# One shared PSUM bank in an attention kernel: its uses moved from the even step to the odd step behind the products with v, and a prologue over four banks

## The reference, cut to what matters

```python
x_proj = x @ Wqkv + bqkv                       # x is the normalised input, 512 tokens at a time
q = x_proj[:, :, :C].reshape(B, n_head, T, hd)          # n_head 16, hd 16: a reshape, not a transpose
k = x_proj[:, :, C:2 * C].reshape(B, n_head, T, hd)
v = x_proj[:, :, 2 * C:].reshape(B, n_head, T, hd)
att = jnp.einsum('bhtd,bhsd->bhts', q, k) * (1.0 / jnp.sqrt(jnp.float32(hd)))
att = jnp.where(causal, att, -jnp.inf)
att = jax.nn.softmax(att, axis=-1)
y = jnp.transpose(att @ v, (0, 2, 1, 3)).reshape(B, T, C)
out = y @ Wproj + bproj
```

## Time and profile before

| | us |
|---|---|
| median of 3 runs | 4216.47 |
| lowest and highest | 4213.61 to 4221.39 |
| the profiled execution, its own time | 4223.2 |
| its span, first to last instruction | 4221.3 |
| PE busy | 3870.2 |
| DVE busy | 2988.6 |
| ACT busy | 2260.9 |
| POOL busy | 1381.5 |

### The profile page before, as it was taken

One profiled execution on the slowest core, in us unless ns is written; L12 is line 12 of the kernel. 1 busy time (PEld: TensorE's weight loads), 2 busy tenths in 40 slices (PEclk: granted clock), 3 DMA queues, 4 the chain that ended last, 5 costly groups with the idle time before them and its releaser, 6 DMA issues. The chain is left out here.

```text
span 4221.3 us, 81220 instructions
## 1 busy us (share of the span) xinstructions
PE 3870.2 (92%) x28814; PEld 2530.1 (60%) x28814; DVE 2988.6 (71%) x7504; ACT 2260.9 (54%) x4454; POOL 1381.5 (33%) x1724
## 2 busy tenths in 40 slices
PE   4997899997499999999999999999999996899997
PEld 4886666674255555555555555555555553667664
DVE  6997467575287777777777777777778773457575
ACT  0110465664156666666666666566656664466664
POOL 2332142333524243243433324333343320133332
PEclk8999899998789999999999999999999998899999
DMA  1332111111677676866767766676666741112111
GB/s 56 99 99 95 40 61 60 51 51 53 115 96 121 101 102 104 114 104 100 116 100 115 107 105 109 94 116 100 103 108 102 101 73 47 41 51 64 47 56 45
DMA packets 701475, 361.54 MB, mean 86 GB/s; under 512 B 305072, under 2 KB 668080, under 8 KB 701104
## 3 DMA queue, kind: packets, MB, share of 16 engines
q1 hardware_dynamic: 701104, 356.65, 47.0%
HBM read 204.49 MB, written 150.99 MB: 84 GB/s over the span
## 5 line engine op out<-in xcount | busy, mean ns | idle before, releaser
L1583 DVE TENSOR_REDUCE att_maxima<-att_s 128x1 f32<-128x512 f32 (+3 forms) x3072 | 1523.1, 550 | 418.8 <-PE att_s L1759 222.7
L1681 ACT ACTIVATE att_probs<-att_s 128x512 f32<-128x512 f32 (+1 forms) x2560 | 1330.9, 556 | 892.4 <-PE att_s L1759 526.7
L1813 PE MATMUL att_s<-att_qs,att_ks 49*128 49x512 f32 (+3 forms) x3072 | 1005.3, 403 | 70.3 <-DVE att_maxima L1583 42.3
L1789 PE MATMUL att_s<-att_ks,att_qs 48*128 48x512 f32 (+3 forms) x3072 | 1003.2, 411 | 3.0 <-DVE att_maxima L1583 1.6
L1813 PEld LDWEIGHTS att_s<-att_qs,att_ks 49*128 49x128 f32 x3072 | 477.4, 187 | 631.2 <-ACT att_probs L1681 404.3
L1841 PE MATMUL att_o_ps<-att_probs,att_vs 128*32 128x512 f32 (+3 forms) x6144 | 638.3, 501 | 2.5 <-issue 2.0
L1759 PE MATMUL att_s<-att_mask,att_places 64*128 64x64 bf16 (+1 forms) x5632 | 595.3, 210 | 0.0
L1789 PEld LDWEIGHTS att_s<-att_ks,att_qs 48*128 48x128 f32 x3072 | 508.4, 189 | 16.8 <-DVE att_maxima L1583 8.6
L1057 PE MATMUL ffn_h2p<-ffn_h,ffn_w 128*128 128x512 f32 x768 | 365.5, 598 | 3.0 <-ACT ffn_h L938 0.9
L1759 PEld LDWEIGHTS att_s<-att_mask,att_places 64*128 64x128 bf16 x5632 | 285.9, 97 | 113.0 <-issue 42.8
L1500 POOL TENSOR_TENSOR att_x_res<-att_x_res,att_bp_row 128x512 f32<-128x512 f32 x64 | 81.3, 1280 | 756.8 <-DMA att_x_res<-x 755.4
(11 more groups left out here) (227 smaller groups left out, 5794.0 us busy)
## 6 DMA issues: line engine op xcount, KB each, us to landing
att_staged<-qk_scratch SPq DMA_DIRECT2D x768, 128.0 KB, 7.1
qk_scratch<-att_parts SPq DMA_DIRECT2D x128, 512.0 KB, 2.9
ffn_x<-x SPq DMA_DIRECT2D x64, 512.0 KB, 5.2
ssm_x<-in_L_attn_a_x_dram SPq DMA_DIRECT2D x32, 512.0 KB, 3.9
x<-ssm_y SPq DMA_DIRECT2D x32, 512.0 KB, 2.9
x<-ffn_y SPq DMA_DIRECT2D x32, 512.0 KB, 3.0
att_x<-x SPq DMA_DIRECT2D x32, 512.0 KB, 12.7
v_scratch<-att_v_tok SPq DMA_DIRECT2D x32, 512.0 KB, 3.5
```

The lines of the kernel that those rows point to most:

```text
L1583: last = v.tensor_reduce(maxima_of[p][:, g, blk, 1 if t0 else 0:2 if t0 else 1], s1_ps[(2 * unit + 1 - g) % 3][:, col:col + w], AX.X, ALU.max)
L1681: a(probs[u % 2][2 * g + p][:, 0:n], bank[:, 0:n], ACT.Exp).then_inc(exp_done, 1)
L1789: last = mm(bank[:, col:col + w], rows_of(qs[buf], g, KROWS, p, BT * blk, BT * (blk + 1)), rows_of(ks[buf], g, KROWS, p, t0, t1), start=k ...
L1813: last = mm(bank[:, col:col + w], rows_of(ks[buf], g, SHIFT + 1, p, BT * j, BT * (j + 1)), rows_of(qs[buf], g, SHIFT + 1, p, t0, t1), star ...
```

## The change

On PE, `slot` now makes the products with v first, and then, in the same place of the same odd step, the use of the x bank whose number is `at`. A use is therefore made between the halves g = 0 and g = 1 of step `at`, where it was between those of step at + 1. The task numbers of ACT, DVE, POOL and SP are not changed.

In the prologue the 22 uses rotate over four banks, `x_ps` and the three `s2_ps`, with counters of their own (`low_free`, `v_free`). The statistics and the normalising of the first two x pieces stand ahead of the weights (DVE, first piece only) and of the masks (POOL). The uses of hb 2 are put between the units of the first pass of quad 0, on PE and DVE. On SP the two `move_max` of quad 0 move behind the first and the last `store_part` of hb 2. On POOL `normalise(2, 0)` moves ahead of the second pair of `lay_out`.

```diff
+        prologue_ps = [x_ps, *s2_ps]
...
+        def x_bank(index):
+
+            return prologue_ps[index % len(prologue_ps)] if index < X_PROLOGUE else x_ps
+
...
-                sp.wait_ge(const_ready, 4)
                 for hb in range(3):
                     for j in range(4):
                         store_part(hb, hb % 2, j)
@@
                             if hb < 2:
                                 sp.wait_ge(x_full, 8 * hb + 2)
                                 load_x(hb + 2, hb)
+                            if hb == 0:
+                                sp.wait_ge(const_ready, 4)
                         if j % 2 and hb < 2:
                             load_stack(2 * hb, hb, hb, 0, j // 2)
+                        if hb == 2 and j in (0, 3):
+                            move_max(0, 0, j // 3)
...
-                    if hb == 1:
-                        for p in range(2):
-                            move_max(0, 0, p)
...
-                pool.wait_ge(loaded, 16 * len(loads))
+                pool.wait_ge(mask_zero, 2)
                 normalise(0, 0)
                 normalise(1, 1)
+                make_masks()
+                pool.wait_ge(loaded, 16 * len(loads))
                 for hb in range(2):
                     for side in range(2):
                         lay_out(2 * hb, side, False)
+                    for e in range(2):
+                        v_bias(hb, e, 8 * hb + 6 + e)
                     if hb == 0:
-                        for e in range(2):
-                            v_bias(hb, e, 6 + e)
+                        normalise(2, 0)
                         for side in range(2):
                             lay_out(1, side, False)
...
                 def low(hb, j, index):
                     dve.wait_ge(hi_ready, 6 * hb + j + 1)
+                    bank, freed = x_bank(index), low_free if index < X_PROLOGUE else x_free
...
                 dve.wait_ge(zero_max, 1)
+                prepare(0, 0, 0)
                 dve.wait_ge(loaded, 16 * len(loads))
...
-                prepare(0, 0, 0)
                 prepare(1, 1, 0)
-                for hb in range(3):
+                for hb in range(2):
                     for j in range(6):
                         low(hb, j, 8 * hb + j)
                     if hb == 0:
                         prepare(2, 0, 1)
                 for unit in range(UNITS1):
                     maxima(0, unit)
+                    if unit % 3 == 2:
+                        low(2, unit // 3, 16 + unit // 3)
...
                 def project(hb, s, j, index):
                     if j == 0:
                         pe.wait_ge(xn_ready, hb + 1)
-                    if not isinstance(index, int) or index > 0:
-                        pe.wait_ge(x_free, index)
+                    bank, old = x_bank(index), index - len(prologue_ps)
+                    if index > X_PROLOGUE:
+                        pe.wait_ge(x_free, index - X_PROLOGUE)
+                    elif 0 <= old < X_PROLOGUE - len(prologue_ps) and old % 8 < 6:
+                        pe.wait_ge(low_free, 6 * (old // 8) + old % 8 + 1)
+                    elif 0 <= old < X_PROLOGUE - len(prologue_ps):
+                        pe.wait_ge(v_free, 2 * (old // 8) + old % 8 - 5)
+                    if index < X_PROLOGUE and j == KT:
+                        pe.wait_ge(low_free, 6 * hb + KT)
...
+                            if g == 0 and step % 2 and (step >= 3 or old):
+                                u = (step - 3) // 2
+                                if u >= 0:
+                                    times_v(quad, q, b, u, old)
+                                else:
+                                    times_v(quad - 1, (q - 1) % 4, b if q else b - 1, UNITS2 - 1, True)
                             for n, (at, kind, which) in enumerate(events):
-                                if g == 0 and at == step - 1:
+                                if g == 0 and at == step:
                                     index = x_base(b, q) + n
...
-                            if g == 0 and step % 2 and (step >= 3 or old):
-                                u = (step - 3) // 2
-                                if u >= 0:
-                                    times_v(quad, q, b, u, old)
-                                else:
-                                    times_v(quad - 1, (q - 1) % 4, b if q else b - 1, UNITS2 - 1, True)
...
-                pe.wait_ge(weights_ready, 2)
+                for hb in range(2):
+                    for j in range(8):
+                        if hb == 0 and j == KT:
+                            pe.wait_ge(weights_ready, 2)
+                        project(hb, hb % 2, j, 8 * hb + j)
                 pe.wait_ge(mask_ready, 20)
-                for hb in range(3):
-                    for j in range(8 if hb < 2 else 6):
-                        project(hb, hb % 2, j, 8 * hb + j)
                 for unit in range(UNITS1):
                     for g in (1, 0):
                         pass_one(0, 0, unit, g)
+                    if unit % 3 == 2:
+                        project(2, 0, unit // 3, 16 + unit // 3)
                 for unit in range(LEAD):
                     for g in (1, 0):
                         pass_one(1, 1, unit, g)
+                pe.wait_ge(low_free, 18)
+                pe.wait_ge(v_free, 4)
                 run(pe, sequence)
```

More of the change, by code:

```diff
@@ L1436, in _ @@
                 g.memset(staged[1][:, :, :], -1.0).then_inc(const_ready, 1)
[L1437 to L1464, removed]
                 def normalise(hb, s):
@@ L1491, in lay_out, with make_masks @@
                     last.then_inc(laid_out[side], 1)
+                def make_masks():
+                    for m in (places[:, :, :], mask[:, :, :, :]):
+                        g.memset(m, 0.0).then_inc(mask_zero, 1)
+                    for s in range(2):
+                        g.memset(vs[s][:, :, HD:32], 0.0).then_inc(mask_zero, 1)
+                    pool.wait_ge(mask_zero, 6)
+                    for s in range(2):
+                        g.memset(vs[s][:, :, HD:HD + 1], 1.0).then_inc(const_ready, 1)
+                    pool.wait_ge(const_ready, 4)
+                    drawn = Chain(pool, mask_ready)
+                    for group in range(2):
+                        rows, row = slice(GROUP * group, GROUP * (group + 1)), slice(GROUP * group, GROUP * group + 1)
+                        for half in range(2):
+                            m = places[rows, half, :]
+                            drawn(g.affine_select(out=m, in_=m, pattern=[[-1, P]], compare_op=ALU.not_equal, fill=1.0,
+                                                  base=GROUP * half, channel_multiplier=1))
+                            m = places[rows, 2 + half, :]
+                            drawn(g.affine_select(out=m, in_=m, pattern=[[1, P]], compare_op=ALU.not_equal, fill=1.0,
+                                                  base=1 - GROUP * (1 + half), channel_multiplier=1))
+                        m = mask[rows, 0, :, :]
+                        drawn(g.affine_select(out=m, in_=m, pattern=[[0, 2], [1, GROUP]], compare_op=ALU.is_ge, fill=-1e30,
+                                              base=0, channel_multiplier=-1))
+                        m = mask[rows, 1, :, :]
+                        drawn(g.affine_select(out=m, in_=m, pattern=[[0, 2], [-1, GROUP]], compare_op=ALU.is_ge, fill=-1e30,
+                                              base=GROUP - 1, channel_multiplier=-1))
+                        drawn(g.memset(places[row, :, :], 0.0))
+                        drawn(g.memset(mask[row, :, :, :], -1e30))
+                        drawn(g.memset(places[row, 0, GROUP:P], 1.0))
+                        drawn(g.memset(places[row, 3, 0:GROUP], 1.0))
@@ L1683, in project @@
                 def project(hb, j, index):
+                    bank = x_bank(index)
                     act.wait_ge(x_full, index + 1)
                     if j < KT:
-                        a(xnT[0][:, j, :], x_ps[:, :], ACT.Copy).then_inc(hi_ready, 1)
+                        a(xnT[0][:, j, :], bank[:, :], ACT.Copy).then_inc(hi_ready, 1)
                     elif j < 6:
@@ L1690, in project @@
                             act.wait_ge(side_stored[j // 2], 32 * hb)
-                        a(parts[:, j, 0, :], x_ps[:, :], ACT.Identity, bias=b_qk[:, j:j + 1]).then_inc(hi_ready, 1)
+                        a(parts[:, j, 0, :], bank[:, :], ACT.Identity, bias=b_qk[:, j:j + 1]).then_inc(hi_ready, 1)
                     else:
@@ L1695, in project @@
                             act.wait_ge(v_stored, 16 * hb)
-                        a(v_tok[:, 2 * e:2 * e + 2, :], x_ps[:, :].rearrange("p (t d) -> p t d", t=2),
-                          ACT.Copy).then_inc(x_free, 1)
+                        a(v_tok[:, 2 * e:2 * e + 2, :], bank[:, :].rearrange("p (t d) -> p t d", t=2),
+                          ACT.Copy).then_inc(v_free if index < X_PROLOGUE else x_free, 1)
                 def turned(r, index):
```

(4 more changed lines are left out.)

30 lines of the change are left out of this document (14 added, 16 removed).

## The result

The changed kernel takes 4454.1 us (median of 4 runs, 4449.75 to 4469.85) against 4218.0 us before: 236 us more, a ratio of 1.0569 (95% interval 1.0543 to 1.0595). The forecast was 4410 us with a range of 4250 to 4480 us.

A forecast was written before the change was run, and what follows sets the result against it. PE sets the pace, and the loop through the x bank has no slack. The profiled 4223.2 us + 217 (slots) - 17 (prologue) = 4423, less 6.7 to the median 4416, rounded down to 4410 us; range 4250 to 4480 us.

The forecast's parts named there:

- The loop through the x bank: Slots: from one x bank use through ACT and DVE to the next; after q or k projections 4.38 becomes 5.38 us.
- no slack: Main stretch: the x bank comes free just when PE arrives, loop 4.38 us against PE's own 4.2 to 4.4 us.
- One of my own signs: Slots: prediction is wrong if ACT's high part starts less than 2 us after the use has ended.
- The price in the slots: Main stretch: 14.9 us lost a batch over 14.55 batches, 217 us, bounds 110 and 265 us.
- the places that ACT alone frees: Slots: 7 places a batch after a v projection or a turned y, 0.4 us lost in all.
- The prologue: Before the slots: new order and four banks take 17 us off, bounds 5 and 28 us.
- 8 + 3 = 11: Prologue: 8 us from normalising ahead of POOL's masks, 3 us from first uses on four banks instead of one.
- the sign that I named for it: Prologue, SP: step is wrong if the moves of the maxima don't start ahead of 1160 us.
- the moves' wait: Prologue, SP: the second half of the moves is freed from its wait for DVE, about 6 us won.
- Faster: Rival: PE has 1.0 us of slack at a use, so the later bank costs nothing; 4180 us, chance 0.12.
- Half the price: Rival: backlogs are worked off during the wait, next halves go by at 0.35 us; 4309 us, chance 0.10.
- An oscillation from period to period: Rival: PE's waits also drop its clock to 1.2 GHz in a tenth of the main stretch; 4560 us, chance 0.06.

The follow-up runs named there:

- e8: Changed kernel with ACT's and DVE's parts between the halves of step at + 1, two halves between use and copy: 4333 us, 1.0279 of the kernel before.
- e3: Changed kernel with ACT's and DVE's parts at step at instead of at + 1, one half between use and copy: 4322 us, 1.0250 of before.
- e7: e2 with ACT's parts at at + 1.25, ahead of the exponential of (at + 1, 1): 4171 us, 0.9888 of the kernel before.
- e2: Changed kernel with the uses back in the even step, so only the prologue is new: 4206 us, 0.9976 of the kernel before.
- e6: Changed kernel with ACT's parts at at + 0.25, between the exponentials of step at, and DVE's at at: 4261 us, 1.0100 of the kernel before.
- e5: Changed kernel with the use behind half g = 1, groups of three and one, parts between the halves of step at + 1: 4246 us, 1.0074 of before.
- e10: e3 with exponentials and maxima on half of the columns, PE's work unchanged, output not the reference's: 4098 us, 0.9729 of the kernel before.
- e11: e2 with both move_max of quad 0 behind load_v of hb 1 again, ahead of hb 2's stores: 4197 us, 0.9960 of the kernel before.
- e12: e7 with both move_max of quad 0 behind load_v of hb 1 again: 4172 us, 0.9909 of the kernel before.

## Why the prediction was right, point by point

- **The loop through the x bank.** Right in its mechanism: the sum of links is 5.22 us in the profile against 5.38 forecast, and with one half less between use and copy (e8) the distance falls to 4.74 us, with two less (e3) to 4.42. The step that it rested on, "no slack", was slightly wrong. There were 0.13 us of it: of the 0.24 us that I counted from the memset to the next use, the signal takes 0.11. And e7 shows that the loop and PE's work only happened to be about equally long; a shorter loop leaves the period as it was. One of my own signs was set badly: ACT's high part starts 1.91 us after the use has ended (2098.03 to 2099.94 us), less than the 2 us that I named, but the forecast's own links give 1.96 us.
- **The price in the slots** was too low: 17.3 us a batch, not 14.9, and 235.8 us from the second step of the first slot to the last half of the last, not 217. These two don't fit by themselves, since 14.55 batches of 17.3 us are 252 us. The first batch and the last two lost 30.4 us, more than the 1.55 full ones that I counted. But the 13 full ones took 33 us more than 13 times 148.2 in the profile before, and only 12 us more than 13 times 165.5 after. A fall of the clock seems to cost the changed kernel less: of two batches at a granted clock of 0.97, the one before takes 154.2 us, 6.0 above 148.2 (1473.60 to 1627.80 us), the one after 169.5, 4.0 above 165.5 (2994.10 to 3163.60 us). By kind, forecast and measured, us a batch: q and k 6.4 and 7.1; transposes of x 2.7 and 3.2; heads 4.8 and 4.2; "out" 1.8 and 1.5; the places that ACT alone frees 0.4 and 1.7; the stretch without uses -1.2 and -0.3. Two of the seven q and k places take 2.6 of the 7.1 us. From 4.34 to 5.69 us: in quad 22 DVE's end of the row maxima (2085.59 to 2086.10 us) stands ahead of the low part. From 5.24 to 6.51 us: this is the seventh place, and the statistics and the longer loop do add up, by 1.3 us where I had allowed 0.1 to 0.4. The rounding down to 4410 us went the wrong way.
- **What failed** is the sentence that "PE's own order still has four halves and one set of products with v from use to use, so the bank is wanted after the same 4.2 us". The amount of PE's work is the same; its order isn't. Four halves in a row overrun three banks. With the loop as short as it was, that costs 6.7 us a batch (e3 against e2), and 6.0 where the copies are earlier in both (e6 against e7); groups of three don't pay it (e5), and it goes with the length of the exponentials and maxima (e10). The loop accounts for the rest, 10.6 us. The two overlap, so after q and k projections the loop hides the fourth half's wait, and where ACT alone frees the bank it shows. That is why 0.4 became 1.7. Where the loop is the longer of the two, as after q and k projections, a forecast by the loop alone stays right; that this is so in most places is luck, since the forecast didn't know the second cause.
- **The prologue.** The second store of q came 10.5 us sooner (1075.18 instead of 1085.66), where 8 + 3 = 11 were forecast: the first transpose 7.5 us sooner (1065.03 instead of 1072.51), and 10.15 instead of 13.15 us from there to the store. So these two terms hold. The failed ones lie on SP, and by the sign that I named for it this step was wrong: the moves of the maxima start at 1162.91 us, not ahead of 1160. Of the 10.5 us, 4.5 were left at the load of v of hb 1 (1158.24 instead of 1162.78): 6 us went in SP's waits between, for landings and for POOL's work behind them, which I had taken to last as long as before; why they lasted longer I didn't test. From that load to the end of the moves it is 19.1 us (1158.24 to 1177.33) instead of 20.2, so of the 6 us for the moves' wait only 1.1 appeared: the store behind the load of v takes 4.12 us of the queue, not the 0.4 I assumed for each (and left out of the sum), and stands ahead of the moves. e11 gets 5.0 us back by moving it.
- **The rivals.** "Faster" is out: PE had no 1 us of slack. "Half the price" is out. The mean granted clock stayed at 0.99 in the main stretch, though PE now idles in most periods. It fell to the 1.2 GHz level for short stretches only, in both kernels: 0.51 from 1470 to 1484 us before, and as much from 1991 to 2005 us after. From the second step of the first slot on there are twelve such stretches after, 61 us together, and five before, 58 us together: more falls, but no more time at that level. An oscillation from period to period, of which the Trainium skill tells ("TensorE: Matmul & The Clock Gate", "A second HAM failure mode"), does not appear in this trace. The distances after a q or k projection follow the place of ACT's copy behind its exponentials: 5.23 us behind three, 4.74 behind two (e8). That agrees with the strict order of ACT's queue which the Trainium skill states ("TensorE: Matmul & The Clock Gate", Part 1).

## What to carry to other kernels

If one engine's order is changed, count for every bank what stands between its filling and its emptying in the other engines' queues, since they don't move with it. Then count how many fillings follow one another without long work between, and hold that against the number of banks: here four in a row on three banks cost 6.0 to 6.7 us a batch, three in a row nothing. And try a copy that a second engine needs ahead of independent work in the first engine's queue; here that alone made the kernel 0.6% faster (e12 against e11).

## What the runs showed of the hardware

- A store issued on SP directly behind the load of v took 4.12 us of the queue, where three others took 1.87 us together. The trace of the kernel before has one such store as well:

```profile
1123.73 0.38 SPq L1340 DMA_DIRECT2D att_vs<-v_scratch  x1
1124.15 4.42 SPq L1316 DMA_DIRECT2D qk_scratch<-att_parts  x1
```

  It stood in the trace from which I forecast 0.4 us each. In e11, with the moves between the load of v and the stores, four stores take 3.08 us together. What holds the store in the queue stays open.
- PE's busy time differs by 8 us (2275.23 and 2283.49 us) for the same 20668 products, while the stretch grows from 2360 to 2596 us, and the granted clock stays at 0.99.
